# The head passes of a decoder layer in another order of steps on all four engines

## What is computed

```python
x = layernorm(x + attn(x))        # 32 query heads, 8 key/value heads of 128, rotary positions, causal, 4-bit weights with scales
x = layernorm(x + xattn(x, ctx))  # 16 heads of 32
x = layernorm(x + ffn(x))         # a dense product and gated low-rank experts
```

```python
w = (qw - 8) * repeat(scales, 128, axis=0)
q, k, v = x @ wq, x @ wk, x @ wv          # then rotary positions on q and k
attn = softmax(causal(q @ k.T / sqrt(128)))
out = (attn @ v) @ wo                      # wo again with scales per group of 128 rows
```

## Time and profile before

| | |
|---|---|
| median of three executions | 769.2 us |
| the profiled execution's own time | 770.07 us |
| its span, first to last instruction | 768.3 us |
| mean granted TensorE clock | 0.984 |
| busy: PE matmuls, PE weight loads | 685.3 us (89%), 449.9 us (59%) |
| busy: DVE, ACT, POOL | 558.1 us (73%), 430.5 us (56%), 432.2 us (56%) |
| mean DMA traffic | 73 GB/s |

### The profile page before, as it was taken

How to read it: one execution, slowest core, us unless ns; L and a number is a source line. 1 busy time by engine, 2 the same in 40 slices (tenths; PEclk the granted TensorE clock), 3 DMA queues, 4 the chain that set the end, 5 groups by cost and what they waited for, 6 DMA issues and landing times. The chain is left out here.

```text
span 768.3 us, 11016 instructions
## 1 busy us (share of the span) xinstructions
PE 685.3 (89%) x3344; PEld 449.9 (59%) x3360; DVE 558.1 (73%) x864; ACT 430.5 (56%) x1190; POOL 432.2 (56%) x379
## 2 busy tenths in 40 slices
PE   4588999999999999999999999996899889968994
PEld 2365766767667676676766767655455443336651
DVE  5757788887888888888888888883343139999455
ACT  2256958659577595775957759576323534612100
POOL 3849688697877968869778796682120000002102
PEclk9889999999999999999999999999999999999997
DMA  8435632341251333234125122122010000020002
GB/s 285 124 85 138 192 114 55 97 124 31 80 140 40 74 111 78 56 96 124 37 75 149 32 67 66 45 73 93 1 55 1 1 1 1 0 86 2 1 0 109
DMA packets 29468, 56.45 MB, mean 73 GB/s; under 512 B 4705, under 2 KB 4961, under 8 KB 28898
## 3 DMA queue, kind: packets, MB, share of 16 engines
q1 hardware_dynamic: 29410, 55.76, 25.4%
HBM read 32.67 MB, written 2.10 MB: 45 GB/s over the span
## 5 line engine op out<-in xcount | busy, mean ns | idle before, releaser
L907 DVE SCALAR_TENSOR_TENSOR arena<-ps,arena 128x512 f32<-128x512 f32 x288 | 214.6, 745 | 42.8 <-ACT arena L647 23.7
L1219 PE MATMUL ps<-x_hi,w_sb 128*128 128x512 f32 x384 | 177.4, 462 | 36.8 <-DVE x_lo L889 17.5
L935 DVE SCALAR_TENSOR_TENSOR y<-ps,arena,y 128x512 f32<-128x512 f32 x192 | 140.7, 743 | 20.2 <-PE ps L1280 17.9
L1219 PE MATMUL ps<-x_lo,w_sb 128*128 128x512 f32 x384 | 154.0, 401 | 0.0
L647 ACT ACTIVATE arena<-ps,arena 128x512 f32<-128x512 f32 x96 | 67.1, 699 | 111.2 <-PE ps L1219 100.8
L514 POOL TENSOR_TENSOR arena<-arena,consts 128x512 f32<-128x512 f32 x80 | 104.3, 1303 | 41.0 <-DVE arena L907 41.0
L520 POOL TENSOR_TENSOR arena<-arena,consts 128x512 f32<-128x512 f32 x80 | 103.5, 1293 | 41.9 <-DMA arena<-arena 41.5
L1219 PEld LDWEIGHTS ps<-x_hi,w_sb 128*128 128x128 f32 x384 | 73.9, 192 | 83.2 <-issue 36.7
L1280 PE MATMUL ps<-heads_hi,wo_sb 128*128 128x512 f32 x256 | 119.1, 465 | 3.7 <-DVE y L935 1.5
L530 POOL TENSOR_TENSOR arena<-arena 128x512 f32<-128x512 f32 x80 | 103.2, 1290 | 7.3
L538 POOL TENSOR_TENSOR y<-arena,y 128x512 f32<-128x512 f32 x64 | 82.1, 1283 | 42.7 <-ACT arena L690 42.2
(11 more groups left out here) (116 smaller groups left out, 946.2 us busy)
## 6 DMA issues: line engine op xcount, KB each, us to landing
arena<-arena SPq DMA_DIRECT2D x160, 128.0 KB, 2.3
arena<-in_qkv SPq DMA_DIRECT2D x48, 256.0 KB, 4.0
arena<-in_o SPq DMA_DIRECT2D x32, 256.0 KB, 3.9
arena<-in_x_t SPq DMA_DIRECT2D x8, 256.0 KB, 5.3
y<-in_x SPq DMA_DIRECT2D x4, 512.0 KB, 4.2
arena<-in_ctx_t SPq DMA_DIRECT2D x4, 512.0 KB, 5.7
out<-y SPq DMA_DIRECT2D x8, 256.0 KB, 2.2
arena<-in_wk SPq DMA_DIRECT2D x1, 1024.0 KB, 5.1
```

What stands on the lines that cost most here:

```text
L907: nc.vector.scalar_tensor_tensor(acc, product_bank(f"G{KC * c + g}"), scale_of(p // 2, c, g), acc, ALU.mult, ALU.add).then_inc(dve_scaled, 1)
L935: nc.vector.scalar_tensor_tensor(dst, by_tile(out_bank(p, u)), out_scale_of(p // 2, u), dst, ALU.mult, ALU.add).then_inc(out_added, 1)
L1219: mm = nc.tensor.matmul(product_bank(f"G{u}"), w_sb[:, c, g, :], part[:, g, half * HALF:(half + 1) * HALF], start=(k == 0), stop=(k == 1))
```

## The change

The steps of `phase(f)` are put in another order on POOL, ACT, DVE and PE; `PRODUCTS` follows. No step is added or removed. Three waits are adapted: the turning bank's users wait for whoever had it before in the new list `TURNS` (the values' turning now stands first in that list and its wait is found by `wait_turn_bank`), and a ring slot is freed by both `times_cos` and `times_sin`, since the cosine no longer comes first always.

The three others after the change, beside the helper that is new:

```diff
+TURNS = "V T0 T1 T2 T3".split()
+        def wait_turn_bank(f, name):
+            at, body = TURNS.index(name) - 1, f
+            while body >= -1:
+                if at < 0:
+                    at, body = at + len(TURNS), body - 1
+                if TURNS[at] == "V" and -1 <= body < LAST:
+                    wait(nc.tensor, v_ready, body + 2)
+                    return
+                if TURNS[at] != "V" and body >= 0:
+                    wait(nc.tensor, probs_t_ready, BPH * body + int(TURNS[at][1:]) + 1)
+                    return
+                at -= 1
...
             elif c >= RING:
+                wait(eng, cos_done, rope_index(p, c - RING) + 1)
                 wait(eng, sin_done, rope_index(p, c - RING) + 1)
             elif p > 0:
+                wait(eng, cos_done, rope_index(p - 1, c + RING) + 1)
                 wait(eng, sin_done, rope_index(p - 1, c + RING) + 1)
```

More of the change, by code:

```diff
@@ L54 @@
 PRODUCTS = (
-    "G0 G1 G2 G3 G4 O0 G5 O1 G6 G7 O2 G8 O3 G9 G10 O4 G11 O5 G12 O6 G13 G14 O7 G15 O8 G16 G17 O9 G18 O10 G19 "
-    "G20 O11 G21 O12 G22 O13 G23 O14 O15").split()
+    "G0 G1 G2 G3 G4 G5 G6 G7 O0 O1 O2 O3 G8 O4 G9 G10 G11 O5 G12 G13 O6 O7 G14 G15 O8 G16 G17 G18 O9 G19 G20 "
+    "G21 O10 G22 O11 O12 G23 O13 O14 O15").split()
+TURNS = "V T0 T1 T2 T3".split()
 def wait(eng, sem, value):
@@ L561, in weights, with outs @@
                         convert(c)
-                def outs(u):
+                def outs(*products):
                     if f > 0:
-                        add_part(f - 1, u)
+                        for u in products:
+                            add_part(f - 1, u)
+                weights(0)
+                outs(3)
+                sine(0)
                 cosine(0)
-                sine(0)
-                weights(0)
+                weights(1)
                 total(0)
-                weights(1)
-                outs(3)
-                weights(2)
                 cosine(2)
                 sine(2)
+                weights(2)
+                total(2)
                 weights(3)
-                total(2)
                 outs(7)
                 cosine(3)
+                cosine(4)
                 sine(3)
-                weights(4)
                 total(3)
-                cosine(4)
-                outs(11)
                 sine(4)
-                weights(5)
                 total(4)
@@ L589, in phase @@
                 sine(5)
+                total(5)
+                outs(11)
+                weights(4)
                 outs(15)
-                total(5)
+                weights(5)
             for c in range(NT):
@@ L743, in phase @@
                 scale_groups(1)
+                exp(0)
+                outs(3)
                 scale_groups(2)
-                outs(3)
-                weights(0)
[L747 to L758, removed]
+                norm(0)
+                copy_values()
+                exp(1)
+                copy_turned(0)
+                norm(1)
+                scale_groups(3)
+                exp(2)
+                outs(7)
+                copy_head(0)
+                exp(3)
+                scale_groups(4)
+                copy_turned(1)
+                weights(0)
                 norm(2)
-                scale_groups(4)
                 copy_head(1)
+                scale_groups(5)
+                copy_turned(2)
                 norm(3)
-                copy_turned(2)
-                scale_groups(5)
-                weights(1)
                 outs(11)
@@ L768, in phase @@
                 copy_turned(3)
+                weights(1)
                 weights(2)
                 copy_head(3)
+                weights(3)
                 outs(15)
-                weights(3)
             phase(-1)
@@ L1314, in phase @@
                 groups(0, 0, 1, 2, 3)
[L1315 to L1320, removed]
+                groups(1, 0, 1, 2, 3)
+                outs(0, 1)
+                score(0)
+                outs(2, 3)
                 groups(2, 0)
-                outs(3)
-                score(0)
                 score(1)
-                groups(2, 1)
+                outs(4)
                 turn_values()
[L1327 to L1331, removed]
+                groups(2, 1, 2, 3)
                 outs(5)
```

74 lines of the change are left out of this document (33 added, 41 removed).

## The result

The changed kernel takes 741.5 us, the median of four executions (739.9 to 742.5), against 769.1 for the kernel before on the same chip: a ratio of 0.963, with a 95% interval of 0.961 to 0.965. It is 3.7% faster. The profiled execution took 742.49 us with a span of 740.7, 27.6 less than the 768.3 before.

What follows compares the result with a forecast made beforehand. PE was taken to lose 3.57 us per pass to waits. 28.52 + 1.15 + 0.25 + 0.15 = 30.1 us per full pass, 25.3 less over 14, plus 4 at the end, gave 740 us; range 728 to 750.

Steps and rivals of the forecast that it cites:

- the likeliest case: The whole kernel: 740 us, own range 728 to 750, chance 0.61.
- The start of a pass: PE no longer stalls before G0, but burst G0 to G7 waits for its readers: cost 1.15 us per pass, 0.25 more on the mean.
- the stall of 0.89: PE's idle time at the pass start until DVE has read O13: goes, 1.0 us with its restart.
- The scores: Score 0 at 5.8 us after the pass start, last rotation done at 4.9: cost nothing.
- The margin of 0.9: Time in us between POOL's last rotation and score 0; if gone, PE waits with all behind score 0.
- the 3.57 us of waits before: PE's loss per full pass in the old kernel: 31.91 us taken against 28.34 without any stall.
- The middle: Attention, values' turning and cosine waits in a pass: all met, cost nothing, with 0.15 us for slips.
- The rival of the narrow waits: PE stops at turn 0, turn 2, weigh 3 and G21: 31.0 us per pass, 753 us; chance 0.16.
- POOL ends last: Rival: late copies delay total(5), score 0 waits 1 us in odd phases: 747 us, in both kinds 754; chance 0.14.
- the signs of being wrong: PE's first wait for POOL in full passes, turn or weighing weight loads waiting for ACT, POOL idle before tile 5's sine.
- The closed loop through POOL: Rival: score 0, ACT's and POOL's outs(3), rotations and next score 0 form a slower loop: 777 us; chance 0.06.
- Phase 15: Last phase: 3 to 6 us less, 4 taken, for the earlier score 0 and about half of the tail.

Runs made afterwards that it cites:

- Alternation: Changed kernel with the first eight products as G0 G4 G1 G5 G2 G6 G3 G7 and DVE's additions of the two tiles in turn: 734.4 us.
- The moved conversion: Changed kernel with ACT converting the last output-weight tile in the next phase, behind the first two scalings: 737.2 us.
- the second experiment: Changed kernel with ACT's weights(3) behind outs(15), as in the kernel before: 741.6 us.
- experiments 8, 9 and 11: Changed kernel, score 0 next to score 1, DVE's outs(1, 2) and ACT's outs(3) earlier: 763.7 us; plus DVE's inv(0) later: 758.9; plus alternating burst: 750.6.
- The fifth experiment: Changed kernel with PE doing output products 2 and 3 before score 0 in the last phase: 740.6 us.
- the fourth experiment: Changed kernel with POOL's outs(11) in front of the last rotation: 749.3 us.
- the last kernel: Changed kernel with the alternating burst, the conversion in the next phase, and O2 and O3 before score 0 in phase 15: 731.0 us.

## Why the prediction was right, point by point

The forecast was 740 us with its own range of 728 to 750; 741.5 was measured, faster, as the likeliest case said.

**The start of a pass.** Right: no idle time before G0, and a burst limited by its readers. O0 was forecast at 4.8 and came at 4.66 in even passes and 5.23 in odd ones. Against the 3.7 of an unhindered burst that is 0.98 and 1.55, on the mean 1.27; I had 1.40. Alternation brought O0 to 3.80 in even passes, which shows that the additions' dependence is the larger part of the 0.98 there; the pass became 0.58 shorter by it. The moved conversion took the 0.58 of odd passes.

**What removing the stall is worth** I had read too simply. I booked the stall of 0.89 as gone and the burst as a new cost. Putting the cut back cost 0.5 us in five even passes and nothing in the nine others: a stall at the front of a burst that is bound by its readers is partly or wholly made good inside it. The sum of the two was right, as it went from a base of PE's steps and not from the stall.

**The scores.** The last rotation was forecast at 4.9 after G0 and ended at 4.86; score 0 at 5.8, measured 5.82. The margin of 0.9 is shown by the run in which 1.25 us of other work came in front of it and 0.4 to 0.7 appeared in four of the five even passes that had no wait before (1.3 in the fifth). That the scores' place carries most of the gain was not in my text: I booked it at nothing, with 0.18 more for the switches between kinds of matmul. It fills PE for 1.03 us while DVE works off what the burst left it, so that O3 finds G7 read; and it starts the attention chain early enough that turn 0 isn't held up. Without it the other moves give nothing in the queues laid out for the early score (768.5 us), and 11 us once three queues are adapted (758.9 against 769.75). My sum was right all the same, because it builds a pass from PE's steps in the new order. It never says where the 3.57 us of waits before lay beyond the 0.89 and what takes each of them away; that they would go was the outcome of the layout by hand, and the runs bear it out.

**The middle.** 28.52 + 1.27 = 29.79 against a mean pass of (29.60 + 30.15)/2 = 29.88: 0.09 of slips, where I took 0.15. The rival of the narrow waits did not come: in full passes the only waits of PE with a bracket are those for POOL.

**POOL ends last.** This rival came in two passes of fourteen. POOL's timeline in phase 1, two sines that wait for swapped copies, and in phase 7:

```profile
98.97 1.30 POOL L537 TENSOR_TENSOR arena<-arena,consts 128x512 f32<-128x512 f32 x1 [1.59 <-DMA arena<-arena]
...
103.26 1.30 POOL L537 TENSOR_TENSOR arena<-arena,consts 128x512 f32<-128x512 f32 x1 [0.34 <-DMA arena<-arena]
...
283.20 1.29 POOL L537 TENSOR_TENSOR arena<-arena,consts 128x512 f32<-128x512 f32 x1 [1.25 <-DMA arena<-arena]
```

They cost PE 1.46 and 0.75 us at the following scores, and made these two passes 1.4 and 0.7 us longer. Two of the signs of being wrong that the prediction gives are there, each in few passes: a wait of PE for POOL in full passes, in two, and idle time of POOL before the sine of tile 5, in three (the 0.34 and 1.25 above and 0.27 at 462.21). In phase 1 SP also loads the second block's context, 512 KB behind each of four turning pairs; that these loads hold the copies up is likely, but no run takes them away. Why a copy is 1.25 us late in phase 7 and at most 0.6 in the odd phases around it is open. The closed loop through POOL didn't appear.

**The sum of the passes.** From the G0 of phase 1 (67.77 us before, 68.78 after) to the start of phase 15 (515.09 before, 489.34 after, where PE could have gone on from the last product of phase 14) the 14 passes took 447.3 and 420.6 us: 26.8 less, where I had 25.3. By the copies it is 1.89 per pass; phase 1 alone went from 33.0 to 30.3. The start took 1.0 us more, the edge of the forecast's -1 to +1; in the traces of the ten kernels whose burst isn't alternated and that have the new order this G0 stands between 67.35 and 68.86 us, so it may be chance. 26.8 and 1.8 for phase 15, less 1.0, are the 27.6 of the span.

**Phase 15 is the term that was mis-sized.** I took 4 us and it gave 1.8 in the profiled execution: it lasted from 489.34 to 518.13, 28.8 us, where it was 30.6. PE's timeline:

```profile
490.63 0.50 PE L1290 MATMUL ps<-heads_hi,wo_sb 128*128 128x512 f32 x1 [1.13 <-DVE heads_lo L944]
...
494.66 1.91 PE L1247 MATMUL ps<-arena 128*128 128x128 f32 x8 [2.83 <-POOL arena L547]
496.22 0.77 PE L1290 MATMUL ps<-heads_hi,wo_sb 128*128 128x512 f32 x1
496.79 0.63 PE L1290 MATMUL ps<-heads_lo,wo_sb 128*128 128x512 f32 x1
...
498.52 1.85 PE L1247 MATMUL ps<-arena 128*128 128x128 f32 x8
...
501.81 0.50 PE L1290 MATMUL ps<-heads_hi,wo_sb 128*128 128x512 f32 x1 [0.99 <-DVE y L953]
```

Score 0 came 5.3 after the start of the phase instead of 7.0, 1.65 us of the 2.0 forecast. From there to the end it took 23.5 us, before 23.6 (522.06 to 545.69). So the other half, the shorter tail, didn't come. What my sum had no term for is the clock behind the wait: score 0, two products and score 1 stand at the 1.2 GHz level here (granted clock 0.50 from 494.6 to 499.8), and before, score 0 and much of score 1 did. The kernel of the second experiment has the same steps in the same order in phase 15, but the level came back sooner, before O3's first matmul (495.15); its timeline, with the first matmul behind the phase:

```profile
492.60 1.91 PE L1247 MATMUL ps<-arena 128*128 128x128 f32 x8 [2.82 <-POOL arena L547]
...
495.15 0.40 PE L1290 MATMUL ps<-heads_hi,wo_sb 128*128 128x512 f32 x1
...
514.67 3.67 PE L1378 MATMUL ps<-arena 128*128 128x512 f32 x8 [0.98 <-ACT arena L708]
```

From score 0 to the end that is 22.1 us, 1.4 less with no other difference than the clock in the trace, and from turn 0 on all its starts in the phase are 1.4 us ahead. So PE's pace does reach the end of this phase, through score 1 and what follows from it. In experiments 8, 9 and 11, where no score of the phase is slow and ACT has outs(3) in front of exp(0), it took 20.9 to 21.1. The fifth experiment gave the first two scores their pace back but has the third at half pace: 22.8. How much of the 2.4 us down to 21.1 is the clock's and how much that order of ACT's isn't shown; 1.4 is the clock's at least in these two traces.

**The page on busy time.** PE's busy time fell by 12.9 us and the span by 27.6; the estimate from busy time was 749, that from starts 740. The Trainium skill (Perfetto Trace Analysis, Identifying the Most-Contended Engine) calls matmul busy time a poor measure of what is left, and this trace agrees.

## What to carry to other kernels

Lay a new order of in-order queues out as a whole, with start-to-start times per engine, and judge it by the sum: single moves don't add up here, as pairing two scores again took back all of it and moving one cut back cost a fifth of a microsecond per pass. Long work for the busiest engine that needs no bank of the ring (a score here) belongs right behind a burst whose readers fall behind, and a chain of operations that build on each other is better taken in turn with another chain. Where a wait of TensorE gets longer, look for the lower clock behind it: here it cost more than the wait's own length in phase 2 of the fourth experiment and 1.4 us in phase 15.

## What the runs showed of the hardware that I had not expected

Waits of 2.60 and 2.83 us of PE had the 1.2 GHz level behind them (a score of eight matmuls 1.68 and 1.91 us long, a product's matmul 0.63), one of 2.26 (phase 2 of the last kernel), one of 1.77 and one of 1.46 had not: the scores behind them ran at full pace, 1.05 us. In the run with the wait of 1.77 the level fell later, at a third score behind two more waits of 0.42 and 1.53 us. So 1.1 us more of waiting, on top of 1.46, cost 2.7. Nor does the low level last equally long behind the same steps: behind score 0 of phase 15 it held for about 5 us in the changed kernel and for 2.5 in the second experiment. What sets that, and what lies between 2.26 and 2.60 us, the runs don't settle.
